# Graph network, attention layer: a fixed scale for the fp16 queries and keys, and turned heads finished over four steps

## The reference

```python
h = jnp.maximum(_layernorm(x, axis=-1), 0.0)
q = (h[rows] @ qW).reshape(e, 4, 24)
k = (h[cols] @ kW).reshape(e, 4, 24)
v = (h[cols] @ vW).reshape(e, 4, 24)
scores = jnp.clip(jnp.einsum('ehd,ehd->eh', q, k), -10.0, 10.0)
exp_s = jnp.exp(scores)
norms = segment_sum(exp_s, rows)[rows]
res = segment_sum((exp_s / (norms + 1e-08))[:, :, None] * v, rows)
x = x + res.reshape(nvar, 96)
```

## Time and profile before

| | us |
|---|---|
| median of 3 runs | 5379.78 (5372.93 to 5381.93) |
| profiled execution | 5377.47, its span 5375.6 |
| TensorE busy | 4309.1 (80% of the span) |
| VectorE busy | 3568.5 (66%) |
| ScalarE busy | 2644.4 (49%) |
| GpSimd busy | 2889.1 (54%) |
| mean granted TensorE clock | 0.893 |

### The profile page before, as it was taken

How to read it: one execution, slowest core, us unless ns; L and a number is a source line. 1 busy time by engine, 2 the same in 40 slices (tenths; PEclk the granted TensorE clock), 3 DMA queues, 4 the chain that set the end, 5 groups by cost and what they waited for, 6 DMA issues and landing times.

```text
span 5375.6 us, 95943 instructions
## 1 busy us (share of the span) xinstructions
PE 4309.1 (80%) x35389; PEld 2642.6 (49%) x35389; DVE 3568.5 (66%) x5464; ACT 2644.4 (49%) x4219; POOL 2889.1 (54%) x2968
## 2 busy tenths in 40 slices
PE   4877799989998666666666666665699999999999
PEld 2777789989997333333333333333533333333333
DVE  6899943343435555555555555554699999999998
ACT  4766610010101333333333333332499999999998
POOL 3100000000002777777777777776188888888887
PEclk9999999999998777777777877777799999999999
DMA  3233379969895444444444444443021121111121
GB/s 71 120 155 143 155 278 344 343 243 363 302 373 189 128 136 129 136 130 136 130 135 134 131 135 130 136 129 92 15 63 58 58 59 58 58 57 54 54 58 38
DMA packets 296270, 759.99 MB, mean 141 GB/s; under 512 B 81000, under 2 KB 183464, under 8 KB 289704
## 3 DMA queue, kind: packets, MB, share of 16 engines
q1 hardware_dynamic: 217352, 595.36, 31.3%
q0 software_dynamic: 78624, 160.79, 11.0%
HBM read 589.77 MB, written 166.22 MB: 141 GB/s over the span
## 4 chain that ended last, share of the span: by engine, by line
DVE 30%; POOL 29%; PE 16%; issue 13%; DMA 9%; DVEq 1%; ACT 1%; SPq 0%; POOLq 0%; ACTq 0%
POOL GA L747 28%; DVE VA L2275 21%; PE p_e L1118 7%; DMA GA<-adj 4%; DMA VA<-adj 4%; PE p_e L1250 2%; PE p_tr L1265 2%; PE p_mm L1035 1%; POOL VA L747 1%; DVE R L1787 1%; DVE M L1789 1%; DVE GA L1789 1%; DVE VA L1787 1%; DVE R L1789 1%; DVE GA L1787 1%
## 5 line engine op out<-in xcount | busy, mean ns | idle before, releaser
L747 POOL DMA_INDIRECT GA<-table_mg,VA x1568 | 1498.2, 955 | 1546.1 <-DMA table_mg<-VA 1043.1
L845 POOL TENSOR_SCALAR VA<-VA 128x1024 f32<-128x1024 f32 (+1 forms) x1204 | 1253.4, 1041 | 307.4 <-ACT VA L1552 209.6
L2275 DVE TENSOR_TENSOR VA<-VA,p_mm 128x2048 f32<-128x2048 f32 x602 | 1370.6, 2281 | 69.2 <-POOL VA L845 36.5
L1156 PE MATMUL p_e<-GA,C 128*128 128x384 f32 x896 | 562.8, 803 | 695.8 <-DMA GA<-table_mg,VA 695.8
L1156 PEld LDWEIGHTS p_e<-GA,C 128*128 128x128 f32 x896 | 272.5, 319 | 960.3 <-DMA GA<-table_mg,VA 764.1
L1552 ACT ACTIVATE VA<-p_e,score_unit 128x1024 f32<-128x1024 f32 x602 | 669.6, 1112 | 86.0 <-PE p_e L1250 43.6
L2076 DVE TENSOR_TENSOR M<-GA,p_mm 128x1344 f32<-128x1344 f32 x112 | 174.1, 1555 | 771.1 <-ACT GA L1500 771.0
L1265 PE MATMUL p_tr<-VA,GA 128*32 128x512 f32 (+1 forms) x5096 | 647.5, 586 | 5.0 <-ACT GA L1564 3.1
L1500 ACT ACT_TABLE_LOAD x112 | 143.7, 1283 | 927.7 <-PE p_e L1156 927.7
L2102 DVE SCALAR_TENSOR_TENSOR R<-R,keep,M 128x97 f32<-128x97 f32 x1568 | 513.6, 328 | 125.4 <-issue 10.7
L1250 PE MATMUL p_e<-T,GA 32*128 32x512 f16 x4632 | 489.5, 382 | 8.3 <-DVE VA L2263 5.8
(11 more groups left out here) (267 smaller groups left out, 7080.9 us busy)
## 6 DMA issues: line engine op xcount, KB each, us to landing
GA<-adj SPq DMA_DIRECT2D x98, 800.0 KB, 6.1
VA<-adj SPq DMA_DIRECT2D x98, 800.0 KB, 6.0
run_m<-R SPq DMA_DIRECT2D x112, 700.0 KB, 3.9
GA<-adj SPq DMA_DIRECT2D x98, 768.0 KB, 6.2
VA<-adj SPq DMA_DIRECT2D x98, 768.0 KB, 6.0
H<-adj SPq DMA_DIRECT2D x56, 896.0 KB, 5.1
adj<-GA SPq DMA_DIRECT2D x25, 1568.0 KB, 5.2
adj<-VA SPq DMA_DIRECT2D x24, 1568.0 KB, 5.1
```

Source lines behind the costliest of these rows:

```text
L747: pool.indirect_dma_start(out=to, out_offset=None, in_=of, in_offset=bass.IndirectOffsetOnAxis(ap=at, axis=0)).then_inc(s, 16)
L845: pool.tensor_scalar(e, e, HIGH, LOW, ALU.min, ALU.max).then_inc(clipped, 1)
L1156: pe.matmul(p_h[k][0:CH, 0:4 * D].rearrange("p (a f) -> p a f", a=2), C[0:CH, C_ID:C_ID + CH], G[0:CH, h, 2 * k:2 * k + 2, 0:2 * D], start ...
L2275: dve.tensor_tensor(e, e, p_mm[n % 2][:, 0:cols_of(n)].unsqueeze(1).to_broadcast([P, HEADS, cols_of(n)]), ALU.mult).then_inc(weighed, 1)
```

## The change

The powers of two for q and k go away, and with them `score_unit`. Both are scaled by a constant, 64, and the exponentials by 64 to the -2, as numbers in the instructions. The start checks instead that no entry of qW and kW is above 4 in size and adds the outcome to the flag, so that larger weights take the general way. In the attention the transposed heads are copied from PSUM to a new SBUF place (`heads_t`) by ScalarE between its second and third exponential of step FIRST_A[b] + 3, which frees the bank; `finish_heads` reads the copy, and its four instructions, each behind a drain, follow the multiplications of four steps.

```diff
+HEADS_TOP, HEADS_UNIT = 4.0, 64.0
...
+        heads_t = VA[:, after + P // 2 + GRP * D:after + P // 2 + GRP * D + SB]
...
                     act.activation(qT[g][:, 0, 0:across(g)], p_e[2 * (g % 2)][:, 0:across(g)], ACT.Identity,
-                                   scale=scales[:, Q_SCALE, 0:1]).then_inc(firsts_ready, 1)
+                                   scale=HEADS_UNIT).then_inc(firsts_ready, 1)
...
-                    act.activation(e[:, 0:2, :], p_pair[:, :, 0:cols], ACT.Exp, scale=score_unit[:, 0:1]).then_inc(exps_ready, 1)
+                    act.activation(e[:, 0:2, :], p_pair[:, :, 0:cols], ACT.Exp, scale=HEADS_UNIT ** -2).then_inc(exps_ready, 1)
                     act.wait_ge(scores_ready, 2 * n + 2)
...
+                    act.activation(e[:, 2, :], p_e[2][:, 0:cols], ACT.Exp, scale=HEADS_UNIT ** -2).then_inc(exps_ready, 1)
+                    if b and n == FIRST_A[b] + LAG:
+                        keep_heads(b - 1, n)
+                    act.activation(e[:, 3, :], p_last[n % 2][:, 0:cols], ACT.Exp, scale=HEADS_UNIT ** -2).then_inc(exps_ready, 1)
...
                 move_heads(GROUPS - 1)
+                keep_heads(GROUPS - 1, len(STEPS_A) + LAG)
+
+            def keep_heads(b, n):
+                act.wait_ge(heads_turned, b + 1)
+                act.activation(heads_t[:, 0:across(b)], p_last[(n + 1) % 2][:, 0:across(b)], ACT.Copy
+                               ).then_inc(heads_used, 1)
...
+            dve.wait_ge(inputs_landed, 16 * n_inputs)
+            heads = WEIGHTS.index("L3_gnn_qW")
+            dve.tensor_reduce(limits[0:D, 0:1], W[:, heads:heads + 2, :].rearrange("p n f -> p (n f)"), AX_X, ALU.max,
+                              apply_absolute_value=True)
             dve.tensor_reduce(flags[0:QG, 3:4], deg_n.rearrange("p s k -> p (s k)"), AX_X, ALU.add)
             dve.drain()
-            dve.tensor_tensor(flags[0:QG, 2:3], flags[0:QG, 2:3], flags[0:QG, 3:4], ALU.subtract).then_inc(flags_ready, 1)
+            dve.tensor_tensor(flags[0:QG, 2:3], flags[0:QG, 2:3], flags[0:QG, 3:4], ALU.subtract)
+            dve.drain()
+            dve.scalar_tensor_tensor(out=flags[0:D, 2:3], in0=limits[0:D, 0:1], scalar=HEADS_TOP, in1=flags[0:D, 2:3],
+                                     op0=ALU.is_gt, op1=ALU.add).then_inc(flags_ready, 1)
...
-                for k, w in enumerate((5, LAYERS_B, LAYERS_B + 1)):
-                    dve.tensor_scalar(inner, bounds_w[:, w:w + 1], 2.0 ** -60, None, ALU.max)
-                    op = powers_of_two(inner, limits[0:1, 4 + 2 * k:6 + 2 * k])
-                    dve.drain()
-                op.then_inc(maxima_ready, 1)
+                dve.tensor_scalar(inner, bounds_w[:, 5:6], 2.0 ** -60, None, ALU.max)
+                powers_of_two(inner, limits[0:1, 4:6]).then_inc(maxima_ready, 1)
                 dve.wait_ge(maxima_turned, 3)
-                for k, n in enumerate((0, 3, Q_SCALE, K_SCALE)):
+                for k, n in enumerate((0, 3)):
                     dve.tensor_copy(scales[:, n, :], p_top[:, 2 * P + 2 * k:2 * P + 2 * k + 2])
                 dve.drain()
-                dve.tensor_tensor(score_unit[:, :], scales[:, Q_SCALE, 1:2], scales[:, K_SCALE, 1:2], ALU.mult)
...
-            def finish_heads(b):
+            def finish_heads(b, part):
 
                 n_t = len(tiles_of(b))
-                dve.wait_ge(heads_turned, b + 1)
...
+                sums = heads_t[:, 0:n_t * P].rearrange("p (t e f) -> p t e f", t=n_t, e=HEADS)
                 of = X[:, GRP * b:GRP * b + n_t, :]
+                dve.drain()
+                if part == 0:
+                    dve.wait_ge(heads_used, b + 1)
+                    dve.tensor_scalar(rec[:, 0:n_t, :], sums[:, :, :, DH], 1e-8, None, ALU.add)
+                if part == 1:
+                    dve.reciprocal(rec[:, 0:n_t, :], rec[:, 0:n_t, :])
+                if part == 2:
+                    dve.tensor_tensor(done_t[:, 0:n_t, :].rearrange("p t (e f) -> p t e f", e=HEADS), sums[:, :, :, 0:DH],
+                                      rec[:, 0:n_t, :].unsqueeze(3).to_broadcast([P, n_t, HEADS, DH]), ALU.mult)
+                if part == 3:
+                    dve.tensor_tensor(of, of, done_t[:, 0:n_t, :], ALU.add).then_inc(out_ready, 1)
...
-                    if b and n == FIRST_A[b] + LAG - 1:
-                        finish_heads(b - 1)
-                finish_heads(GROUPS - 1)
+                    if b and LAG <= n - FIRST_A[b] < LAG + 4:
+                        finish_heads(b - 1, n - FIRST_A[b] - LAG)
+                for part in range(4):
+                    finish_heads(GROUPS - 1, part)
```

More of the change, by code:

```diff
@@ L180, in build @@
         tops = sb("tops", [P, TILES])
-        scales = sb("scales", [P, CONVS + 2, 2])
-        score_unit = sb("score_unit", [P, 1])
+        scales = sb("scales", [P, CONVS, 2])
         dinv_s = sb("dinv_s", [P, TILES])
@@ L999, in turn_limits @@
                 pe.wait_ge(maxima_ready, 3)
-                pe.matmul(p_top[:, 2 * P:2 * P + 8], C[0:1, C_TRI:C_TRI + P], limits[0:1, 2:10], start=True, stop=True
+                pe.matmul(p_top[:, 2 * P:2 * P + 4], C[0:1, C_TRI:C_TRI + P], limits[0:1, 2:6], start=True, stop=True
                           ).then_inc(maxima_turned, 1)
@@ L1539, in dense_heads @@
                     act.activation(qT[g][:, 0, 0:across(g)], p_e[2 * (g % 2)][:, 0:across(g)], ACT.Identity,
-                                   scale=scales[:, Q_SCALE, 0:1]).then_inc(firsts_ready, 1)
+                                   scale=HEADS_UNIT).then_inc(firsts_ready, 1)
                     act.activation(kT[:, 0, g * SB:g * SB + across(g)], p_e[2 * (g % 2) + 1][:, 0:across(g)], ACT.Identity,
-                                   scale=scales[:, K_SCALE, 0:1]).then_inc(firsts_ready, 1)
+                                   scale=HEADS_UNIT).then_inc(firsts_ready, 1)
                 at["mm"] += GROUPS
@@ L1917, in bound_weights @@
                 first = WEIGHTS.index(BOUNDED[0])
[L1918 to L1921, removed]
+                dve.tensor_reduce(limits[0:D, 0:n_top - 1], W[:, first:first + n_top - 1, :], AX_X, ALU.max,
                                   apply_absolute_value=True)
@@ L2237, in dense_heads @@
                     nodes = slice(g * SB, g * SB + across(g))
-                    for k, (to, scale, ready) in enumerate(((qT[g][:, :, 0:across(g)], Q_SCALE, q_ready),
-                                                            (kT[:, :, nodes], K_SCALE, k_ready))):
+                    for k, (to, ready) in enumerate(((qT[g][:, :, 0:across(g)], q_ready), (kT[:, :, nodes], k_ready))):
                         dve.wait_ge(firsts_ready, 2 * g + k + 1)
                         dve.scalar_tensor_tensor(out=to[:, 1, :], in0=p_e[2 * (g % 2) + k][:, 0:across(g)],
-                                                 scalar=scales[:, scale, 0:1], in1=to[:, 0, :], op0=ALU.mult,
+                                                 scalar=HEADS_UNIT, in1=to[:, 0, :], op0=ALU.mult,
                                                  op1=ALU.subtract).then_inc(ready, 1)
@@ L2251, in dense_heads @@
                 dve.drain()
-            def finish_heads(b):
+            def finish_heads(b, part):
                 n_t = len(tiles_of(b))
-                dve.wait_ge(heads_turned, b + 1)
-                turned_at = FIRST_A[b + 1] + LAG
-                sums = p_last[(turned_at + 1) % 2][:, 0:n_t * P].rearrange("p (t e f) -> p t e f", t=n_t, e=HEADS)
-                dve.tensor_scalar(rec[:, 0:n_t, :], sums[:, :, :, DH], 1e-8, None, ALU.add)
+                sums = heads_t[:, 0:n_t * P].rearrange("p (t e f) -> p t e f", t=n_t, e=HEADS)
+                of = X[:, GRP * b:GRP * b + n_t, :]
                 dve.drain()
-                dve.reciprocal(rec[:, 0:n_t, :], rec[:, 0:n_t, :])
-                dve.drain()
-                dve.tensor_tensor(done_t[:, 0:n_t, :].rearrange("p t (e f) -> p t e f", e=HEADS), sums[:, :, :, 0:DH],
-                                  rec[:, 0:n_t, :].unsqueeze(3).to_broadcast([P, n_t, HEADS, DH]), ALU.mult
-                                  ).then_inc(heads_used, 1)
-                dve.drain()
-                of = X[:, GRP * b:GRP * b + n_t, :]
-                dve.tensor_tensor(of, of, done_t[:, 0:n_t, :], ALU.add).then_inc(out_ready, 1)
+                if part == 0:
[8 more added lines that the diff above has]
+                    dve.tensor_tensor(of, of, done_t[:, 0:n_t, :], ALU.add).then_inc(out_ready, 1)
             def attention():
```

8 lines of the change are left out of this document (2 added, 6 removed).

## The result

The changed kernel took 5324.01 us (median of 6 runs, 5305.29 to 5334.43), the kernel before beside it 5377.86 us (median of 6, 5372.93 to 5384.1): a ratio of 0.9895 (95% interval 0.9876 to 0.9913), 54 us faster where I had forecast 23. Its profiled execution took 5315.89 us, with a span of 5314.1. The direction was right and the time lies in the range, but the gain is that of the first rival ("the period falls further", 5326 us), not of my forecast.

The account below looks back on a forecast made before the run. Two rings of waits in the attention, both 2.35 us a step, were taken as the bound; 15 + 5 + 2 + 1.8 - 0.4 = 23 us gained gave 5355 us, 8-in-10 range 5320 to 5380.

Parts of the forecast that it names:

- first rival: Attention steps: hidden slack lets the period fall to 2.27 us, 52 us gained, 5326 us in all; chance 14%.
- The fixed scale in the attention: Exponentials without the scale operand: 0.027 us saved in each of 554 attention steps, 15 us.
- Three-step ring: Attention waits from mask through scores, first exponential, clip and multiplication to the mask three steps on: 7.05 us, forecast 6.97.
- two-step ring: Attention waits through first and second exponential, last scores and value sums, without VectorE and GpSimd: 4.70 us, forecast 4.54.
- The operand's price: Scale operand on each ScalarE exponential: taken as 0.08 us, from rows that differ by 76 ns.
- The group changes: Finishing heads at 12 attention group changes: 3.6 us lost each instead of 4.0, 5 us gained.
- The parts: VectorE's four finish instructions, each behind a multiplication at a group change: 3.26 us in all.
- the first delay: At a group change VectorE's multiplication waits for GpSimd's second clip, behind the third exponential: 0.9 us.
- The clock at the changes: TensorE's granted clock: 0.86 at the third change before, explaining 4.15 us against 3.0; full clock expected after.
- The smaller parts: Outside the attention steps: q and k copies gain 2 us, the start 1.8, the last finish loses 0.4.
- the new reduction: At the start, reduction and comparison of some 0.6 us, covered by VectorE's 6.60 us DMA wait.
- The copy on the path to the end: One copy more in the last finish: 0.4 us at most lost.

Follow-up runs that it names:

- number_second: The changed kernel with the scale operand back on the first and third exponential, so only the second has a number; 5643.80 us, ratio 0.9951.
- number_third: The changed kernel with the scale operand back on the first and second exponential, so only the third has a number; 5654.66 us, ratio 0.9979.
- copy_after: The changed kernel with ScalarE's copy of the heads moved behind the third exponential of its step; 5607.22 us, ratio 0.9893.
- finish_only: The kernel before, scale operands kept, with the heads copied off PSUM and finished over four steps; 5665.89 us, ratio 0.9988.
- both: The changed kernel with the heads' copy behind the third exponential and the heads' product and addition on GpSimd; 5309.75 us, ratio 0.9875.
- after: The changed kernel itself, with the whole change, against the kernel before; 5324.01 us, ratio 0.9895.
- on_pool: The changed kernel with the heads' product and addition on GpSimd, behind its clips of a group's eighth and ninth step; 5599.29 us, ratio 0.9879.
- scale_only: The changed kernel with the heads finished in one piece out of PSUM as before, leaving the fixed scale alone; 5615.00 us, ratio 0.9903.
- after_again: The changed kernel unaltered, run again on the same chip as the last kernels for comparison; 5321.76 us, ratio 0.9907.

## Why the prediction was right or wrong, point by point

**The step that failed: "The fixed scale in the attention".** It took "Three-step ring: 7.05 - 0.08 = 6.97". Measured: steps of 2.268, a ring of 6.80. The two rings, side by side, were the right ones, but the three-step ring had one stretch wrong: the term for what it loses was 0.08 and should have been 0.25, so the step's 0.027 us were 0.083. I had closed the ring with "clip 1.19 later, multiplication 2.31 later" and taken that stretch, with its clip pair of 2.20 us, as GpSimd's own. It held a wait for the third exponential. So all three exponentials lie in the ring: 0.09 for the first, and for the second and third 0.15, until the pair's own 2.05 us takes over: 7.05 - 0.09 - 0.15 = 6.81, against 6.80 measured. number_second (6.96 where my ring would have stayed at 7.05) and the pairs of 2.20, 2.11 and 2.05 us show it; number_third is 6.96 by this ring too, and is held by the two-step ring instead. A row of before, ScalarE in the step of the earlier trace rows, which I did not look at, said so:

```profile
4103.72 0.69 ACT L1555 ACTIVATE VA<-p_e,score_unit 128x512 f32<-128x512 f32 x1
```

It ends at 4104.41, while the first clip, from 4103.33 for 1.04 us, is done at 4104.37: the second clip was not late for want of GpSimd.

The two-step ring was forecast at 4.54 and measured at 4.52, so the first rival's 2.27 was right to the hundredth, also in that both rings end there. That rival's condition, hidden slack in the three-step ring, was what the traces show.

**The operand's price** was 0.084 to 0.089, not 0.076: 0.003 us a step, 2 us in all.

**The group changes.** I had 3.6 us a change and measured 4.2, no gain in place of 5 us. The parts came as forecast: 12.01 - 8.76 = 3.25 us against 3.26, with both large parts at 1.2 us. This is the lock that the Trainium skill describes ("SBUF — State Buffer", "Who interferes with whom"); the traces agree with it: the product takes 1.24 us when a clip has started before it, and 0.56 when it starts together with one, which then takes 1.46 us in place of 1.04 (copy_after). The 0.6 between is the first delay (1.00 against 0.9), the shorter step that the change is measured against (four of 2.268 are 9.07, I had 9.3), and a stall of VectorE of 0.31 to 0.38 us, which I had not seen: seven of the ten periods take 115.41 to 115.49 us and three, 0.35 less, 115.11 to 115.12, which makes 0.24 a group. 0.10 + 0.23 + 0.24 = 0.57.

**The clock at the changes.** I had read one change at 3.0 us and nine at 4.15. In truth two ran at the full clock, at 3.0 and 2.9 us (118.18 and 118.01), and the eight after them at 0.86, at 4.3 on average. The clock came back as forecast, and it was worth about 1.3 us a change; but against the old finish at the full clock the new one costs 0.9 us more beside the old step (finish_only) and 1.0 to 1.3 more beside the new one. The comparison that I made, 4.0 against 3.6, mixed the two.

**The smaller parts** held: the head copies 12 x 0.18 = 2.2 us (forecast 2), the start 1.7 (1.8), the new reduction hidden (nothing). The copy on the path to the end took 0.28 us.

**The sum.** 49 + 2.2 + 1.7 - 0.3 = 53 us; the medians say 54. Of the forecast 23 the steps and changes together made 15 + 5 = 20, where 49 was measured; those 29 are the error. The steps alone are 554 x 0.083 = 46 us, 31 more than forecast. The ten regular changes gave nothing; the other 3 us lie at the last two changes and in the first and last group. The profiled executions differ by 61.6, of which some 8.5 are chance ahead of the attention (below).

## What to carry to other kernels

A merged row of two instructions on one engine is a duration of the engine only if it is twice one of them: 2.20 against 2 x 1.04 less the overlap was a wait, and whoever feeds the second instruction was in the ring. When the cycle time of a pipeline is worked out, follow each instruction to the one that came last among its inputs, for every instruction of the ring, and compare the ends to the hundredth. A saving measured beside one step time need not add to another that changes the step: run each half alone. And before the cost of an event is averaged over its repeats, look at the granted clock of each.

## What the runs showed of the hardware that was not expected

- VectorE's stream of multiplications stops for 0.31 to 0.38 us with no releaser but issue, at 4039.09, 4179.52, 4319.92, 4460.35 in the changed kernel, each 140.4 us after the last; the next that shows is 275.3 us on. In both, with two VectorE instructions fewer a change, the distance is mostly 143.5 us. In group periods it is 1.217 in after and also in copy_after (139.2 us in 114.42), which has the same VectorE program, and 1.260 in both and on_pool (143.7 in 114.08). So it seems to go with the count of instructions rather than with time; its cause stays open.
- A VectorE product or sum of two SBUF operands of 128x384 took anything from 0.56 to 1.44 us, by how it fell against GpSimd's clips, and a clip that it met took up to 1.46 us in place of 1.04. Moving a copy on a third engine by one place was enough to go from one to the other.
- On GpSimd the product of 128x384 took 0.84 us and the sum 1.00, nearly as long as a clip of 128x1024 (1.04); on VectorE the product took 0.56 where it did not have to wait for a clip.
- The granted clock fell at some changes and not at others of the same kernel, though TensorE was idle equally long ahead of both (1.46 and 1.47 us in scale_only).
- Profiles of one chip put the attention's start anywhere between 3883 us (after_again) and 3908 us (both), for kernels that are the same up to there, while the attention's length of one kernel repeated to 0.2 us (1413.8 and 1413.6). In these profiles the spread of the totals comes from ahead of the attention; a change in the attention is better read from its length.
